# Two edits to the start of a three-stage tower: weight loads issued one by one, and two fields gathered by whole rows

## The reference

```
e  = stack([tbl_f[ids[:, f]] for f in range(8)], axis=1)          # 512 x 8 x 1024
t  = tanh(relu(e[:, not_idx] @ Wn1 + bn1) @ Wn2 + bn2)             # replaces those fields: iv
pair_fuse(pairs, W1, b1, W2, b2) = relu(concat(iv[p0], iv[p1]) @ W1 + b1) @ W2 + b2
z  = (sum over and_pairs + sum over or_pairs + remaining fields) / count
h  = relu(concat(z, dense_ctx) @ W_top1 + b_top1); h = relu(h @ W_top2 + b_top2); y = h @ W_top3
```

## Time and profile before

| | |
|---|---|
| median of 3 runs | 546.09 us (546.03 to 551.28) |
| the profiled execution | 546.39 us, of which span 544.6 us |
| mean granted TensorE clock | 0.987 of full speed |
| TensorE matmuls busy | 529.3 us |
| VectorE, ScalarE, GpSimd busy | 365.1, 248.4, 251.2 us |

### The profile page before, as it was taken

One profiled execution on the slowest core, in us unless ns is written; L12 is line 12 of the kernel. 1 busy time (PEld: TensorE's weight loads), 2 busy tenths in 40 slices (PEclk: granted clock), 3 DMA queues, 4 the chain that ended last, 5 costly groups with the idle time before them and its releaser, 6 DMA issues.

```text
span 544.6 us, 6205 instructions
## 1 busy us (share of the span) xinstructions
PE 529.3 (97%) x2378; PEld 439.3 (81%) x2378; DVE 365.1 (67%) x371; ACT 248.4 (46%) x301; POOL 251.2 (46%) x208
## 2 busy tenths in 40 slices
PE   6699999999799999999999999999999999999998
PEld 6698888888578888888888788888888888888885
DVE  5268899999596675788646687842423684578732
ACT  3374667555256553534445645331325342224343
POOL 5508878898427635031087107888856700000000
PEclk9889999999989999999999999999999999999999
DMA  7917786673986676358189535833499933232000
GB/s 234 345 54 173 153 222 196 190 164 107 184 154 174 142 117 186 81 81 153 36 166 301 156 102 159 253 105 104 113 235 267 231 95 108 86 105 64 1 0 1
DMA packets 39632, 78.95 MB, mean 145 GB/s; under 512 B 7377, under 2 KB 7633, under 8 KB 39602
## 3 DMA queue, kind: packets, MB, share of 16 engines
q0 software_dynamic: 19648, 40.93, 34.1%
q1 hardware_dynamic: 19522, 37.51, 22.7%
q10 hardware_dynamic: 432, 0.11, 0.1%
HBM read 86.90 MB, written 0.00 MB: 160 GB/s over the span
## 4 chain that ended last, share of the span: by engine, by line
PE 73%; POOL 16%; issue 3%; DMA 3%; ACT 2%; another core or an unknown queue 2%; DVE 1%; ACTq 0%
PE PS L1104 71%; POOL XR L498 13%; POOL WR L520 2%; DMA WR<-weights 2%; DMA XR<-table,rows 1%; PE PS L1265 1%; PE PS L1131 1%; ACT XO L705 0%; DVE WO L825 0%; ACT WO L617 0%; DMA XR<-ints 0%; PE PS L1272 0%; ACT XR L676 0%; POOL XR L487 0%
## 5 line engine op out<-in xcount | busy, mean ns | idle before, releaser
L1104 PE MATMUL PS<-XO,WO 128*128 128x512 f32 (+1 forms) x2256 | 507.9, 387 | 8.8 <-DVE WO L825 4.4
L1104 PEld LDWEIGHTS PS<-XO,WO 128*128 128x128 f32 x2256 | 420.1, 190 | 95.2 <-DVE WO L825 5.3
L617 ACT ACTIVATE WO<-WR 128x1024 fp32r<-128x1024 f32 x93 | 98.6, 1060 | 239.4 <-PE PS L1104 213.7
L825 DVE TENSOR_TENSOR WO<-WR,WO 128x1024 fp32r<-128x1024 f32 x93 | 113.8, 1224 | 132.3 <-ACT WO L617 119.2
L498 POOL DMA_INDIRECT XR<-table,rows x96 | 127.6, 1329 | 60.7 <-issue 28.3
L647 ACT ACTIVATE XO<-XR 128x1024 fp32r<-128x1024 f32 (+1 forms) x76 | 79.3, 1046 | 3.0 <-DVE XR L973 3.0
L520 POOL DMA_DIRECT2D WR<-weights x30 | 37.5, 1676 | 91.4 <-DVE WO L825 48.0
L904 DVE TENSOR_TENSOR XO<-XR,XO 128x1024 fp32r<-128x1024 f32 x60 | 73.2, 1221 | 1.0 <-ACT XO L647 0.5
L584 POOL DMA_INDIRECT XR<-table,rows_rest x32 | 54.0, 1686 | 15.1 <-issue 7.9
L921 DVE STREAM_TRANSPOSE XR<-XR 128x1024 f32<-128x1024 f32 x26 | 55.9, 2148 | 0.0
L973 DVE TENSOR_TENSOR XR<-XR 128x1024 f32<-128x1024 f32 (+1 forms) x32 | 38.7, 1219 | 0.0
(11 more groups left out here) (73 smaller groups left out, 126.6 us busy)
## 6 DMA issues: line engine op xcount, KB each, us to landing
WR<-weights SPq DMA_DIRECT2D x71, 512.0 KB
WR<-weights POOLq DMA_DIRECT2D x30, 512.0 KB, 8.6
XR<-XR POOLq DMA_DIRECT2D x32, 64.0 KB, 4.9
XR<-table,rows POOLq DMA_INDIRECT x110, 5.0
XR<-table,rows_rest POOLq DMA_INDIRECT x32
XR<-dense_t SPq DMA_DIRECT2D x3, 32.0 KB, 3.0
XR<-w_dense SPq DMA_DIRECT2D x3, 32.0 KB, 3.1
XR<-ints SPq DMA_DIRECT2D x1, 84.0 KB, 2.2
```

The costliest lines, as they stand in the source:

```text
L617: nc.scalar.activation(WO[:, n % 2, 0, :], WR[:, slot, :], ACT.Copy).then_inc(w_hi, 1)
L825: V_.tensor_tensor(WO[:, n % 2, 1, :], WR[:, raw_slot(n), :], WO[:, n % 2, 0, :].bitcast(FP32), ALU.subtract).then_inc(w_lo, 1)
L1104: mm = nc.tensor.matmul(PS[:, bank, cols], WO_t[:, slot, ws, i, k, :], XO[:, x0 + k, xs, cols], start=first and k == 0 and n == 0, stop=la ...
```

## The change

SyncE issues its third to seventh load each behind a wait for rows that land, in place of two and three at once. GpSimd gathers fields 2 and 3 as four DMAs of whole rows each (into buffers 6 and 7), and SyncE moves each field by 16 DMAs inside the core's memory into the staging that the transposes read (buffers 5 and 6). GpSimd waits for field 3's moves before it gathers field 4, SyncE for field 2's moves before those of field 3. VectorE works out the row numbers of fields 2 and 3 with fewer columns, those of fields 4 to 7 later, and makes the two sums L844 behind all parts of x of entry 0 and no longer between them.

```diff
-        rows0 = sb("rows0", [P, 2, BT], INT32)
+        rows0 = sb("rows0", [P, 4, BT], INT32)
...
+        FIELD_ROWS = {2: 6, 3: 7}
+        def row_quarter(slot, p, c):
+            return flat(FIELD_ROWS[slot])[p:p + 32, :].rearrange("p (b x) -> p b x", b=BT)[:, :, c:c + QC]
+        def staged_quarter(slot, p, c):
+            return flat({2: 5, 3: 6}[slot])[p:p + 32, :].rearrange("p (b x) -> p b x", b=BT)[:, :, c:c + QC]
...
@@ SyncE @@
             for b in range(2):
                 sp.wait_ge(x0_in[b], 16)
+            load(2)
             for h in range(2):
+                if h == 0:
+                    sp.wait_ge(x0_in[3], 16)
+                else:
+                    sp.wait_ge(x1_in[1], 16)
                 sp.dma_start(raw_piece(2 + h), quadrant_rows(4 + 2 * h, 0)).then_inc(raw_in[2 + h], 16)
-                for b in range(2 * h, 2 * h + 2):
-                    sp.wait_ge(x0_in[b], 16)
-            load(2)
+            sp.wait_ge(field1_in[0], 16 * 4)
             load(3)
+            sp.wait_ge(field1_in[1], 16 * 4)
             load(8)
-            for n, split in ((9, 2), (12, 3), (13, 8), (16, 9), (14, 10), (15, 11), (17, 12), (20, 13), (28, 14),
+            def move_field(slot):
+                sp.wait_ge(field_rows[slot], 16 * BT)
+                for g in range(4):
+                    for q in range(Q):
+                        sp.dma_start(staged_quarter(slot, 32 * q, QC * g), row_quarter(slot, 32 * g, QC * q))\
+                            .then_inc(field_moved[slot], 16)
+            for n, split in ((9, 2), (12, 3)):
+                load_after(n, split)
+            move_field(2)
+            for n, split in ((13, 8), (16, 9), (14, 10), (15, 11)):
+                load_after(n, split)
+            sp.wait_ge(field_moved[2], 16 * 4 * Q)
+            move_field(3)
+            for n, split in ((17, 12), (20, 13), (28, 14),
...
@@ GpSimd @@
+            def gather_rows(slot):
+                for b in range(BT):
+                    pool.indirect_dma_start(flat(FIELD_ROWS[slot])[:, H * b:H * (b + 1)], None, table,
+                                            bass.IndirectOffsetOnAxis(ap=rows0[:, slot, b:b + 1], axis=0))\
+                        .then_inc(field_rows[slot], 16)
...
                 gather_quarter(i)
+            pool.wait_ge(rows2_ready, 1)
+            gather_rows(2)
             for h in range(2):
                 add_piece(0, Q6, h)
-            pool.wait_ge(rows2_ready, 1)
-            gather_half(2, 0)
             for h in range(2):
                 add_piece(0, Q7, h)
-            gather_half(2, 1, range(4))
             for h in range(2):
                 add_piece(0, P4, h)
-            gather_half(2, 1, range(4, 8))
-            gather_half(3, 0)
-            gather_half(3, 1)
             pool.wait_ge(setup_done, 1)
+            gather_rows(3)
+            pool.wait_ge(field_moved[3], 16 * 4 * Q)
             gather_half(4, 0)
...
@@ VectorE @@
-            slot_rows(2, 6).then_inc(rows2_ready, 1)
+            for s in (2, 3):
+                last = V_.tensor_tensor(prod_t[:, BT * F * s:BT * F * (s + 1)].rearrange(gf, f=F), row_bf,
+                                        hot_sf[:, s, :].unsqueeze(1).broadcast_to([P, BT, F]), ALU.mult)
+            link(last)
+            link(V_.tensor_reduce(rows0_f[:, 2 * BT:], prod_t[:, 2 * BT * F:].rearrange(gf, f=F), AX.X, ALU.add))
+            V_.tensor_copy(rows0[:, 2:4, :].rearrange("p s b -> p (s b)"), rows0_f[:, 2 * BT:]).then_inc(rows2_ready, 1)
             for h in range(2):
                 x0_lo(h, 0)
                 x0_lo(h, 1)
-                if h:
-                    for i in range(2):
-                        dve.wait_ge(raw_in[2 + i], 16)
-                        V_.tensor_tensor(WR[:, i, :], WR[:, i, :], WR[:, 2 + i, :], ALU.add).then_inc(t1_sum, 1)
                 x0_lo(h, 2)
                 x0_lo(h, 3)
+            for i in range(2):
+                dve.wait_ge(raw_in[2 + i], 16)
+                V_.tensor_tensor(WR[:, i, :], WR[:, i, :], WR[:, 2 + i, :], ALU.add).then_inc(t1_sum, 1)
+            slot_rows(4, 4)
...
+                elif slot in field_moved:
+                    dve.wait_ge(field_moved[slot], 16 * 4 * Q)
```

More of the change, by code:

```diff
@@ L270, in dlrm_tower @@
         row_t = scratch(BT * F)
-        prod_t = scratch(2 * BT * F)
+        prod_t = scratch(4 * BT * F)
         rows_f = scratch((SLOTS - 1) * GROUPS)
-        rows0_f = scratch(2 * BT)
+        rows0_f = scratch(4 * BT)
         hot = scratch(SLOTS * F)
@@ L321, in dlrm_tower @@
         quarter = sem("quarter")
-        field_in = {(s, h): sem(f"field_in{s}_{h}") for s in range(2, SLOTS) for h in range(2)}
+        field_in = {(s, h): sem(f"field_in{s}_{h}") for s in range(4, SLOTS) for h in range(2)}
+        field_rows = {s: sem(f"field_rows{s}") for s in (2, 3)}
+        field_moved = {s: sem(f"field_moved{s}") for s in (2, 3)}
         field1_in = [sem(f"field1_in{i}") for i in range(2)]
@@ L801, in _ @@
             link(last)
-            link(V_.tensor_reduce(rows0_f, prod_t.rearrange(gf, f=F), AX.X, ALU.add))
-            V_.tensor_copy(rows0[:, :, :].rearrange("p s b -> p (s b)"), rows0_f).then_inc(rows0_ready, 1)
+            link(V_.tensor_reduce(rows0_f[:, 0:2 * BT], prod_t[:, 0:2 * BT * F].rearrange(gf, f=F), AX.X, ALU.add))
+            V_.tensor_copy(rows0[:, 0:2, :].rearrange("p s b -> p (s b)"), rows0_f[:, 0:2 * BT]).then_inc(rows0_ready, 1)
             link(V_.scalar_tensor_tensor(out=row4_gf, in0=int_in[:, I_GROUP:I_GROUP + GROUPS * F].rearrange(gf, f=F),
```

## The result

The changed kernel takes 552.23 us (median of 4 executions, 550.43 to 552.63), the kernel before 546.06 beside it (540.98 to 551.28): a ratio of 1.0147, 95% interval 1.0095 to 1.0199. It is slower by 1.5%, clear of the noise, outside the predicted 534 to 551 and on the other side. The profiled execution took 552.14 us (span 550.3, mean clock 0.981), 5.75 more than the one before.

The account below looks back on a forecast made before the run. TensorE was taken as the bound, late only at the start and at 146 us. Profiled 546.39 - 5.5 (start) + 1.0 (later stall) = 541.9, and 541.6 as the median of the runs; range 534 to 551.

Parts of the forecast that it names:

- What bounds the kernel: Whole kernel: TensorE, busy 529.3 of 544.6 us; only its gaps or low clock, at the start and 146 us, can be won.
- I take it that ScalarE's release at 25.04 belongs to this backlog: Start: SyncE's queued loads hold ScalarE's release; with 1.6 MB less ahead it comes between 18.5 and 22.
- The term of 5.5 us: Start: gain from spacing out five loads, taken from a range of 5.0 to 6.3 us.
- Rival 2: Start: field 2's whole-row gathers right behind the quarters delay ScalarE's release to 30 to 32; 551 to 554 us; chance 0.11.
- 99 in place of 98.24: GpSimd's first gather of field 4 waits for field 3's moves and starts at 99 us; bounds 94 and 104.
- rival 4: Field 3's moves are late (104): 547 us with the gain at the start, 552 without it; chance 0.11.
- under the transfer: Field 3's moves: SyncE's 16 issues of about 0.4 us, six to seven us in all, lie hidden under the transfer.
- the term of 9.2: Field 3's moves: 2.10 MB at 228 GB/s takes 9.2 us of transfer.
- The stall of 146 stays and grows by some 1 us: TensorE's wait for stage 1's Q6 adds remains, some 1 us longer; bounds -6.0 and +6.
- Behind it nothing changes: GpSimd after field 4's start: the same 16 gathers, long ones among them, and the same adds.
- A move that is late by more holds VectorE too: VectorE's transposes of field 3 at t = 27: moves hidden by only 1 or 2 us, later ones hold VectorE.
- Field 2's moves and SyncE's later loads: Field 2's 16 moves share engines with Q6's adds; later loads stand 6 us behind moves, issued over 10 us ahead.

Follow-up runs that it names:

- e9: Kernel before with only SyncE's first loads spaced out and VectorE's two sums L844 behind all parts of x: ratio 0.9970.
- e2: Kernel before with only fields 2 and 3 gathered by whole rows and moved, loads and sums as before: ratio 1.0012.
- f2: Changed kernel with field 2's whole-row gathers behind the adds of Q6 and four plain GpSimd DMAs of the same bytes in their old place: ratio 0.9998.
- f1: Kernel before with field 2's first eight quarter gathers ahead of the adds of stage 0's Q6: ratio 1.0068.
- e3: Kernel before with 20 idle products at the start in place of 36: ratio 1.0002.

## Why the prediction was wrong

**What bounds the kernel**: right. TensorE's gaps at the start and near 130 to 150 hold 5.2 of the 5.7 us that the span grew.

**The start, "I take it that ScalarE's release at 25.04 belongs to this backlog"**: this step failed. e9 has the shorter backlog and the same release, 24.45, and in the changed kernel entry 1 came 3.95 us later, not 5.5 sooner. The term of 5.5 us was 0 as far as e9 can tell (ratio 0.9970). The earlier trace rows show the engines full beside the wait, and I took that for its cause; in e2 and f2 they are as full (1.04, 1.03) and TensorE is busy. The "issue" gap in the earlier trace rows said that TensorE itself was short of something, and I read only ScalarE's wait.

**Rival 2, field 2's rows behind the quarters prolong the wait**: this is what happened. It said a release at 30 to 32 and 551 to 554; measured 30.05 and 552.2. It put a loss of 1% at a release behind 30.5; at 30.05 the loss is already larger, since the second one came on top, which it didn't have. So its time is right partly by luck. Its reason ("because that queue ran dry") was close: not the bytes in the queue, but gathers. It was given 0.11, since the step above had the wait tied to the loads.

**Field 4's start, "99 in place of 98.24"**: mis-sized. Measured 4.5 us later against entry 1, that is 102.7 in the old clock, towards rival 4's 104. The term that was short is the landing of field 3's rows: they were issued as said (the last at 84.81, 80.9 in the old clock), but landed 8.1 us behind it, not 5.0, so that the moves began at 89.0 in place of 86. From there to the first gather it is 13.7 us against 13.0 in the sum, and that is partly luck. SyncE's issues took 0.60 us each and one 1.90, 11.6 for sixteen, where 0.4 and "under the transfer" stood; each move landed 2.3 to 3.8 us behind its issue, so none piled up, and the last landed 1.8 behind the end of the issues. The moves were bound by their issue, with the engines not far behind: share 0.9 and 201 to 209 GB/s from 95 to 101. At a full share that is the 228 GB/s of the earlier trace rows again, so the term of 9.2 was sound and hidden under the issues. The Trainium skill gives 189 GB/s for a transfer of 1 MiB over 32 partitions, in "SBUF — State Buffer", section "Door 1: The DMA port swizzle"; the moves of 128 KB, many at a time, ran somewhat above it.

**"The stall of 146 stays and grows by some 1 us"**: the size came out (5.59 against 4.37) for another reason. The stall moved forward to Q5's adds, because a gather in front of them was held; "Behind it nothing changes" was wrong, since the same 16 gathers met VectorE in another phase.

**"A move that is late by more holds VectorE too"**: right, 0.62 us at t = 27, without effect of its own.

**Field 2's moves and SyncE's later loads**: right that no wait of TensorE came from them. Their size was wrong: beside the adds of Q6 and Q7, with the engines full, the sixteen issues took 21.3 us (0.60 to 2.02 each), not six or seven.

## What to carry to other kernels

An idle engine whose releaser had long ended, or TensorE with "issue" gaps, points to who was issuing gathers just then. On the chips that showed it here, four or eight further gathers in front of the start (5 and 10 us of issue) put it off by 4 to 8 us, while plain DMAs of the same bytes cost at most 1 us. Put what TensorE waits for (accumulating DMAs) ahead of gathers on the same engine, with some 8 us to spare, since one gather may be held through a whole run of VectorE's two-operand sums. Price small DMAs inside the core's memory by their issue and by the transfer, and take the longer; beside other traffic on full engines the issues themselves become longer.

## What the runs showed that was not expected

- Starvation of TensorE: ScalarE's wait of 9 us at the start, and TensorE's gaps of 1 to 5 us, on every chip used but one, where four profiles show none. What TensorE is short of (its instructions or its semaphores' updates) and why chips differ stays open: no run here separates them. In the instruction queue one packet of 16 KB runs between 18 and 22 us in starved executions (before, after, e9, f1) and in those that aren't (e2, e3), so this packet alone doesn't make the wait.
- A gather held for over 4 us ends 0.82 or 0.83 us behind the end of VectorE's run of operations with two operands in SBUF, in the eight cases compared.
- A SyncE DMA of 32 partitions inside the core's memory takes 0.60 us to issue where the engines have room (field 3's, share 0.9) and 1.38 in the median where they are full (field 2's); a load of 128 partitions takes 0.37 in the median.
